# Expert offsets read into TensorE's registers in one load per half of the walk

## The reference

```python
logits = jnp.einsum('btd,de->bte', X, Wg) + bg          # 8 experts
topv, topi = jax.lax.top_k(logits, 2)
w = jax.nn.softmax(topv, axis=-1)
xs = X[:, :, None, :] * w[..., None]
for e in range(8):
    h = silu(xs @ W1[e]) * (xs @ W3[e])                 # 128 -> 512
    y = h @ W2[e]                                       # 512 -> 128
    out = out + where(topi == e, y, 0).sum(axis=2)
```

## Time and profile before

| | us |
|---|---|
| device time, median of three runs (lowest to highest) | 968.24 (968.15 to 970.38) |
| span of the profiled execution, first to last instruction | 1000.9 |
| TensorE (PE) busy | 897.1 (90%) |
| its weight loads (PEld) busy | 640.5 (64%) |
| VectorE (DVE) busy | 792.1 (79%) |
| GpSimd (POOL) busy | 734.7 (73%) |
| ScalarE (ACT) busy | 673.5 (67%) |
| mean granted clock of TensorE | 0.978 |

### The profile page before, as it was taken

How to read it: one execution, slowest core, us unless ns; L and a number is a source line. 1 busy time by engine, 2 the same in 40 slices (tenths; PEclk the granted TensorE clock), 3 DMA queues, 4 the chain that set the end, 5 groups by cost and what they waited for, 6 DMA issues and landing times.

```text
span 1000.9 us, 33897 instructions
## 1 busy us (share of the span) xinstructions
PE 897.1 (90%) x13160; PEld 640.5 (64%) x13160; DVE 792.1 (79%) x2394; ACT 673.5 (67%) x1183; POOL 734.7 (73%) x685
## 2 busy tenths in 40 slices
PE   5789999999999879899987899999999985998884
PEld 3467676776777656566654676777677764666663
DVE  6889898888889877777656889888888887866563
ACT  6688888878877626556555787767767762545552
POOL 6789989889887745666545999878888883666662
PEclk9999999999999979999999999999999997999997
DMA  5201011010030001122111000000000001121222
GB/s 153 78 10 45 3 45 45 3 45 2 3 107 3 2 20 39 52 43 85 38 30 51 3 3 3 12 3 2 13 3 3 13 2 30 41 43 44 86 62 82
DMA packets 21118, 33.79 MB, mean 34 GB/s; under 512 B 4578, under 2 KB 10466, under 8 KB 20964
## 3 DMA queue, kind: packets, MB, share of 16 engines
q1 hardware_dynamic: 13728, 18.50, 5.9%
q0 software_dynamic: 5888, 12.07, 4.8%
q10 hardware_dynamic: 1348, 1.05, 0.3%
HBM read 22.44 MB, written 9.18 MB: 32 GB/s over the span
## 4 chain that ended last, share of the span: by engine, by line
PE 63%; DVE 18%; ACT 6%; issue 6%; POOL 3%; another core or an unknown queue 2%; DMA 1%; SPq 0%; POOLq 0%; DVEq 0%; ACTq 0%
PE ps L1698 8%; PE ps L1889 8%; PE ps L1700 8%; PE ps L1699 7%; DVE arena L1308 4%; PE ps L1919 3%; PE ps L2128 3%; PE ps L1853 3%; PE ps L1920 3%; PE ps L1921 3%; PE ps L2140 2%; PE ps L2141 2%; PE ps L2142 2%; PE ps L1864 2%
## 5 line engine op out<-in xcount | busy, mean ns | idle before, releaser
L784 POOL TENSOR_TENSOR arena<-arena 128x1024 f16<-128x1024 f32 x190 | 344.9, 1816 | 86.2 <-ACT arena L980 75.9
L1308 DVE CUSTOM_DVE_ANT_0 arena<-ps,mask_qk 128x512 bf16<-128x512 f32 (+3 forms) x512 | 224.4, 485 | 25.0 <-PE ps L1853 23.8
L972 ACT ACTIVATE arena<-ps,lift 128x1024 f32<-128x1024 f32 (+1 forms) x192 | 186.7, 972 | 85.0 <-PE ps L1899 82.2
L1889 PE MATMUL ps<-arena 64*128 64x512 f16 (+3 forms) x1536 | 148.5, 299 | 10.2 <-ACT arena L972 6.8
L835 POOL DMA_INDIRECT arena<-x_rows,arena x92 | 92.6, 1006 | 88.5 <-PE ps L2103 43.7
L1919 PE MATMUL ps<-arena 128*128 128x65 f16 x1280 | 130.9, 195 | 0.2 <-DVE arena L1332 0.2
L1920 PE MATMUL ps<-arena 128*128 128x64 f16 x1280 | 130.4, 193 | 0.0
L1921 PE MATMUL ps<-arena 128*128 128x65 f16 x1280 | 130.0, 194 | 0.0
L843 POOL DMA_INDIRECT y_rows<-arena x92 | 90.8, 987 | 49.0 <-ACT arena L1138 26.1
L1919 PEld LDWEIGHTS ps<-arena 128*128 128x128 f16 x1280 | 117.4, 98 | 8.4 <-issue 0.5
L1920 PEld LDWEIGHTS ps<-arena 128*128 128x128 f16 x1280 | 117.9, 99 | 0.2 <-issue 0.2
(11 more groups left out here) (288 smaller groups left out, 2695.9 us busy)
## 6 DMA issues: line engine op xcount, KB each, us to landing
stage<-in_L_ffn_W SPq DMA_DIRECT2D x4, 1024.0 KB, 5.3
arena<-y_rows SPq DMA_DIRECT2D x14, 256.0 KB, 3.6
x_rows<-XN SPq DMA_DIRECT2D x8, 256.0 KB, 2.1
arena<-x_rows,arena POOLq DMA_INDIRECT x92
y_rows<-arena POOLq DMA_INDIRECT x92
stage<-in_L_attn_Wkv SPq DMA_DIRECT2D x2, 512.0 KB, 8.3
X<-in_L_attn_tokens SPq DMA_DIRECT2D x3, 256.0 KB, 5.1
out_x<-X SPq DMA_DIRECT2D x3, 256.0 KB
```

Of the source, the lines that this page charges most:

```text
L784: g.tensor_tensor(PL[:, b, :, cols], P32[:, :, cols], PH[:, b, :, cols], ALU.subtract).then_inc(s_pl, 1)
L972: a_.activation(P32[:, :, UNIT_AT[u]:UNIT_AT[u] + UNIT_W[u]], ps[:, 4:6, 0:UNIT_W[u]], ACT.Exp, bias=lift[:]).then_inc(s_ex_p, 1)
L1308: v_.tensor_tensor_reduce(masked[:, x, 0:w], ps[:, 2 + x, at:at + w], mask_qk[:, CH - w:CH], 1.0, NEG, ALU.add, ALU.max, accum_out=MX[:, i ...
L1889: mm(ps[:, 4 + x, at:at + w], keys, queries, start=(n_ == 0 and part == 0), stop=False)
```

## The change

```diff
             def moe(m):
-                pe.wait_ge(s_r_tile, PARTS * m + 1)
-
                 offsets = []
 
-                def load_offsets(t):
-
+                def load_offsets(h):
+
+                    pe.wait_ge(s_r_tile, PARTS * m + h + 1)
                     _, at = nc.values_load_multi_w_load_instructions(
-                        tile_ei[0:1, t:min(t + 8, HT * (t // HT + 1))], engines=(mybir.EngineType.PE,), min_val=0,
+                        tile_ei[0:1, HT * h:HT * (h + 1)], engines=(mybir.EngineType.PE,), min_val=0,
                         max_val=(EXPERTS - 1) * H,
...
                     offsets.extend(at)
                 load_offsets(0)
...
-                    if t % HT % 8 == 5 and t % HT + 3 < HT:
-                        load_offsets(t + 3)
                     if t == HT - 1:
-                        pe.wait_ge(s_r_tile, PARTS * m + 2)
-                        load_offsets(HT)
+                        load_offsets(1)
```

## The result

The changed kernel takes 977.74 us (median of four runs, 976.97 to 978.19) beside 968.19 us for the kernel before (967.79 to 970.38): a ratio of 1.0095, 95% interval 1.0081 to 1.0109, so 9.5 us slower. The forecast was 974.7 us, slower, with a range from 969.3 to 978.2; the measured time lies 0.5 us inside its upper end.

The account below looks back on a forecast made before the run. TensorE (PE), busy 89% in both walks, was taken to bound the kernel. Terms -3.4 + 7.4 + 0 + 3.2 - 0.5 = +6.7 us, scaled to +6.5, gave 974.7 us, range 969.3 to 978.2.

Parts of the forecast that it names:

- What the loads cost: Register loads of line 2092: 0.297 us per group of four words at a multiple of four, 0.244 per single value.
- (1): Removed loads of tiles 5, 13, 28 and 36: -3.4 us over both walks, from -5.0 to -2.5.
- (2): Load behind the first half's last tile grows from 8 to 23 values: +3.7 us each, +7.4 in all.
- (3): Walk's first load grows from 8 to 23 values, 2.2 us, covered by VectorE's late line 1652: no cost.
- One sign of the forecast: Second token's line 2103 should start within 0.2 us of where it did against the walk's start.
- (4): One low-clock stretch behind each of the two long loads: 1.6 us each, +3.2; far end 2.2 each.
- (5): Small waits of the tiles behind the long stall vanish: -0.5 us for both walks together, far end -1.5.
- Rival A: Chance 0.68: the sum of the forecast's terms holds, slower, own range 972 to 978 us.
- B: Chance 0.15: no difference that shows; low clock hidden or absent, all idle of removed loads regained: 969.6 us.
- D: Chance 0.05: flat price per value whatever the place, 0.175 us, so 4.0 us per new load: 973.4 us.
- E: Chance 0.04: cost goes by registers filled, so the first load takes 5.6 us too: about 980 us.
- C: Chance 0.08: faster; the long load at tile 22 isn't paid by singles and takes 2.2 us: 965 us.

Follow-up runs that it names:

- clean execution: The kernel before, unchanged, profiled a second time: span 965.5 us, 1.0012 of the other runs of the same kernel.
- long execution: The first profiled execution of the kernel before, on which the prediction was made: span 1000.9 us beside runs of 968.2 us.
- kernel with this half alone: Against the kernel before, only the first half's 23 offsets in one load ahead of tile 0, second half in three loads: 967.17 us, ratio 0.9993.
- kernel with the second half alone: Against the kernel before, only the second half's 23 offsets in one load behind tile 22, first half in three loads: 977.03 us, ratio 1.0085.
- filled kernel: Changed kernel plus 20 unused matmuls ahead of each long load: 1019.56 and 1017.50 us, ratios 1.0091 and 1.0106 to the kernel before.
- third set: Later set of runs with the kernel before at 1008.05 us; the changed kernel, run again unchanged, took 1018.38 us, ratio 1.0096.
- kernel with two pieces: Changed kernel with the second half read in loads of 12 and 11 values behind tiles 22 and 28: ratio 1.0018 to the kernel before, twice.

## Why the prediction was right, step by step

**What the loads cost.** Right. 23 x 0.244 = 5.6 was 5.46 to 5.55 in the long loads of five runs; five groups and three singles, 2.2, was 2.09 to 2.30. The two prices were read off loads of seven and eight and hold, within 0.13 us, for 3 (0.78 to 0.79, but one took 0.90), 4 (0.34), 11 (2.65), 12 (2.89) and 20 values (1.36 and 1.55). The Trainium skill's 200 ns a register (page "Runtime: NRT & Kernel Launch", section "Instruction fetch mechanics") lies between them: 0.24 off a multiple of four words, 0.10 on it for 23 values.

**(1), the loads that go.** Forecast -3.4, measured -3.55 over the four pieces without the long load. The size is right by luck, the parts are not: the array's idle time behind tiles 28 and 36 of the first walk was 1.48 and 0.16 in the rows read the earlier trace rows, but 0.37 and 0.05 in the clean execution, and in the second walk 0.76 and 0.62 instead of 1.42 and 1.22. What I took off from these rows for VectorE and ScalarE being late belonged to the long execution as well. And I priced a load at the idle time ahead of the transposes, where it costs 0.3 to 0.4 us more at tiles 28 and 36. I took 5.0 of idle time less 1.6; it was 2.1 of idle time and 1.4 beside it.

**(2), the longer load.** Forecast +7.4, measured +7.0. The array stood 4.75 and 4.30 us, where 4.7 and 5.1 were forecast: the 1.44 that the second was built on is 0.79 in the clean execution.

**(3), the first load.** Forecast nothing. The kernel with this half alone gives 0.9993. In the pieces it is +1.0 and -0.7, which sum to 0.3, and neither is the load's: the kernel with the second half alone, whose first load is still of eight values, takes 9.17 and 7.47 us from its first load to tile 2, the changed one 9.17 and 7.49. Against the earlier trace rows line 1652 kept its distance from the first load: 366.78 - 363.40 = 3.4 us there; in the changed kernel

```profile
368.58 0.26 DVE L1652 TENSOR_TENSOR arena<-ps,arena 128x128 f16<-128x128 f32 x1
...
829.88 0.29 DVE L1652 TENSOR_TENSOR arena<-ps,arena 128x128 f16<-128x128 f32 x1
```

it is 3.4 (368.58 - 365.19) and 2.9 (829.88 - 826.94). The slack was just enough in the first walk: ScalarE's copy ended 0.3 us before line 1652 started. One sign of the forecast was too narrow, that the second token's transpose would keep its distance from the load within 0.2 us. The distance is 3.79 and 3.38 us, and 3.79 and 4.63 in the execution that the forecast was made on, 3.22 and 3.96 in the clean one. Again the kernel with the short first load has nearly that of the changed one, 3.79 and 3.32, so it isn't the load that moves it.

**(4), the clock.** This is the term that was mis-sized: forecast 1.6 us a walk from one low stretch of 3.4, measured 2.5 a walk (5.1 in all, as a remainder; 2.2 a walk by the filled kernel), as the low stretch at each load is 6.8 us long, of which 6.0 and 5.5 are work. The forecast took the length of a low stretch from one behind a wait of 1.84 us and assumed it for a wait of 4.7. Its far end, 2.2, was too low as well by the remainder. The Trainium skill, page "TensorE: Matmul & The Clock Gate", section "HAM oscillation — how this bites in real kernels", says that matmuls behind a long enough wait begin at the low clock each time; both long loads agree (0.50 behind each), and moving the word takes both low stretches away.

**(5), catching up.** Forecast -0.5; nothing of it shows behind tile 25. Tiles 25 to 45 run at their 2.51 and 2.96 us, and those of the second walk at 2.52, with or without a stall before. Within the two pieces with the long load the remainder of 5.1 is 0.7 below the estimate of 5.8, so some may be there; no run separates it.

**The sum.** 7.0 + 5.1 - 3.55 = 8.6 against a forecast of 6.7; about 1 us of the span's 9.7 lies ahead of the walk. The missing 2 us are the clock's, +1.9; the load's -0.4 and the +0.5 of catching up that didn't show cancel. The forecast was also scaled by 0.967, as if the long execution were the kernel's own; without that it would be 974.9. Rival A is what happened, 3 us beyond its middle and within 0.3 us of its upper end, 978. B fell with the clock, D and E with the first loads of 2.2 us, and C with the long ones of 5.5. C's working was right where its premise is made true: with a long load of 2.2 us the kernel is faster, but by 1.5 us (0.9985), not by 3.

## What to carry to other kernels

Before loads into a sequencer's registers are merged or split, read where each begins: here a row of offsets that began one word short of a multiple of four cost 0.24 us a value instead of 0.07 to 0.10, and moving it by one word took 11 us from the changed kernel. A load leaves no idle time as long as it is shorter than the work already handed to the array (0.7 to 1.8 us here), so several short ones hide better than one long: off the boundary, two of 2.9 and 2.65 us cost 1.8 us in the whole where one of 5.5 cost 9.7. With loads of 2.3 us and less no further gain can be told. And price a wait of 4.3 to 4.8 us ahead of TensorE at its own length plus up to half of the work that falls into the low clock behind it: 2.2 to 2.6 us here.

## What the runs showed that I had not expected

- The low clock at a wait of 4.3 to 4.8 us lasts 6.8 us (0.50 in 441.7 to 448.5, and the same length at all four long loads of the changed kernel and of the one with the second half alone), twice as long as behind one of 1.84. In the changed kernel's execution of the third set it began about with the wait and lasted 10.2 us.
- The length of a single wait doesn't settle it: in the kernel with two pieces the clock stayed at 1.00 behind one of 2.13 us and fell around one of 1.87 that had others close ahead of it.
- The same kernel took 968 us in some sets and 1008 in others, with narrow spreads in both, and its first profiled execution was 35 us longer than its second. Those 35 us lie in the two walks: tile 0 to 45 takes 136.3 and 123.2 us in the clean execution of the kernel before, 155.9 and 139.8 in the long one. The long ones have ScalarE and GpSimd idle for something that the trace calls remote and doesn't name, which the clean ones of the kernel before and of the changed one lack. The rows of the changed kernel's waits in its long execution (total us, times, longest):

```profile
ACT arena L1130 <- remote: 18.3, 11, 2.6
ACT arena L1138 <- remote: 14.3, 8, 2.3
DVE arena L1662 <- remote: 13.2, 5, 3.0
POOL arena L835 <- remote: 12.6, 9, 1.9
```

What holds them up there stayed open.
